# Projections, attention and routed experts of a two-layer block: statistics earlier, last values last, second product two behind, rows of maxima placed in one hop

## The reference

```python
h = _layernorm(x) * (1 + ca) + sa
Q, K, V = h @ W_q.T, h @ W_k.T, h @ W_v.T
Qr, Kr = _rope(Qh, cos, sin), _rope(Kh, cos, sin)
scores = einsum('bhqd,bhkd->bhqk', Qr, Kr) * DH ** (-0.5)       # causal
heads = einsum('bhqk,bhkd->bhqd', softmax(scores), Vh)
...
a = xf @ W1a_e + b1a_e                                          # for each expert e
b = xf @ W1b_e + b1b_e
y = silu(a) * b @ W2_e + b2_e
acc = acc + w_e[:, None] * y
```

## Time and profile before

| | us |
|---|---|
| median of 3 runs | 2507.34 (2504.72 to 2518.98) |
| the profiled execution | 2501.4 |
| its span | 2499.7 |
| PE busy | 2214.6 (89%) |
| DVE busy | 1692.3 (68%) |
| ACT busy | 1274.4 (51%) |
| POOL busy | 862.8 (35%) |

### The profile page before, as it was taken

One profiled execution on the slowest core, in us unless ns is written; L12 is line 12 of the kernel. 1 busy time (PEld: TensorE's weight loads), 2 busy tenths in 40 slices (PEclk: granted clock), 3 DMA queues, 4 the chain that ended last, 5 costly groups with the idle time before them and its releaser, 6 DMA issues. The chain is left out here.

```text
span 2499.7 us, 38782 instructions
## 1 busy us (share of the span) xinstructions
PE 2214.6 (89%) x12968; PEld 1404.3 (56%) x12968; DVE 1692.3 (68%) x2750; ACT 1274.4 (51%) x2452; POOL 862.8 (35%) x1057
## 2 busy tenths in 40 slices
PE   7876999999999999988999599963999999999991
PEld 5662333333333333326777456652888888888881
DVE  7767887878777787825787778764455555555456
ACT  2220777777766677773233244421455555555552
POOL 3442412213121211212455512444344434445341
PEclk9995999999999999998999798875999999999996
DMA  5389104042241500003000100115534434544326
GB/s 208 126 186 144 26 2 69 7 65 32 40 49 23 70 2 2 2 1 131 1 0 0 33 0 8 37 37 169 175 132 138 140 129 136 174 150 140 131 73 214
DMA packets 130021, 200.23 MB, mean 80 GB/s; under 512 B 13808, under 2 KB 102896, under 8 KB 128432
## 3 DMA queue, kind: packets, MB, share of 16 engines
q1 hardware_dynamic: 113472, 144.32, 17.3%
q0 software_dynamic: 14544, 48.05, 10.7%
q10 hardware_dynamic: 1824, 5.52, 1.3%
HBM read 150.97 MB, written 46.88 MB: 79 GB/s over the span
## 5 line engine op out<-in xcount | busy, mean ns | idle before, releaser
L917 DVE TENSOR_REDUCE tile_max<-p_m 128x2 f32<-128x1024 f32 (+3 forms) x640 | 651.4, 1061 | 146.1 <-PE p_m L779 76.4
L879 ACT ACTIVATE probs<-p_s 128x512 f32<-128x512 f32 (+3 forms) x1280 | 597.2, 535 | 244.9 <-PE p_s L788 240.2
L2143 PE MATMUL p_up<-f_xT,f_w 128*128 128x512 f32 (+1 forms) x2304 | 463.6, 350 | 9.2 <-POOL f_w L2306 9.2
L2143 PEld LDWEIGHTS p_up<-f_xT,f_w 128*128 128x128 f32 x2304 | 368.8, 189 | 59.6 <-issue 9.6
L725 POOL TENSOR_SCALAR_AFFINE_SELECT probs<-probs 128x128 f32<-128x128 f32 x512 | 145.0, 292 | 721.6 <-ACT probs L879 712.6
L775 PE MATMUL p_m<-ka,qa 96*128 96x512 bf16 (+3 forms) x1280 | 361.2, 365 | 30.9 <-PEq L256 18.5
L788 PE MATMUL p_s<-qa,ka 99*128 99x512 bf16 (+3 forms) x1280 | 351.6, 351 | 21.3 <-DMA qa<-max_scr 8.6
L2306 POOL TENSOR_TENSOR f_w<-f_raw,f_w 128x1024 fp32r<-128x1024 f32 x96 | 231.4, 2414 | 398.8 <-ACT f_w L2195 398.8
L802 PE MATMUL p_o<-probs,va 128*32 128x512 f32 (+3 forms) x2560 | 301.1, 541 | 0.3 <-POOL probs L725 0.3
L2158 PE MATMUL p_y<-f_w,f_hidden 128*128 128x256 f32 x1872 | 255.8, 283 | 28.7 <-DVE f_hidden L2260 14.9
L2158 PEld LDWEIGHTS p_y<-f_w,f_hidden 128*128 128x128 f32 x1872 | 237.3, 188 | 50.7 <-issue 31.5
(11 more groups left out here) (269 smaller groups left out, 2575.5 us busy)
## 6 DMA issues: line engine op xcount, KB each, us to landing
f_raw<-in_W1a SPq DMA_DIRECT2D x24, 1024.0 KB, 7.1
f_raw<-in_W1b SPq DMA_DIRECT2D x24, 1024.0 KB, 9.2
f_raw<-in_W SPq DMA_DIRECT2D x24, 1024.0 KB, 11.7
qk_scr<-parts SPq DMA_DIRECT2D x48, 256.0 KB, 2.8
qa<-qk_scr POOLq DMA_DIRECT2D x42, 256.0 KB, 15.6
ka<-qk_scr POOLq DMA_DIRECT2D x42, 256.0 KB, 17.5
v_scr<-wqkv_raw SPq DMA_DIRECT2D x32, 256.0 KB, 3.8
g_ys<-y_rows SPq DMA_DIRECT2D x16, 512.0 KB, 8.7
```

The costliest lines, as they stand in the source:

```text
L879: nc.scalar.activation(probs[:, (buf * UNITS + n) % NPROBS, h, lo:CH], p_s[:, s_bank(("exp", HG * n + h), buf), lo:CH], ACT.Exp, scale=DH ...
L917: nc.vector.tensor_reduce(out=tile_max[:, 2 * hp:2 * hp + 2, i, bank], in_=p_m[:, at_bank, :, 0:width], op=ALU.max, axis=AX.X).then_inc(ma ...
L2143: last = nc.tensor.matmul(p_up[:, f % 2, ab, 0:size], w1[:, wh, ab * KT + kt, f * P:(f + 1) * P], xT[:, t % 2, xh, kt, 0:size], start=(kt, ...
```

## The change

Four things are changed.

- In the projections the statistics of chunk i+2 stand behind `rest_of_hT(i + 1)` on DVE, the keys' two rotations are issued one ahead of and one behind `split(i, 0)`, and POOL's `deviation` stands ahead of the first `split_off`.
- In the last chunk PE multiplies the keys ahead of the values, ACT takes the values between the two roundings of the keys, and SP stores them between the queries' and the keys' parts.
- In the attention `place` is three DMAs straight from the rows in SBUF to the place under the queries, with one semaphore for each of the two row buffers; the scratch rows in DRAM go. ACT's next use of a row buffer waits for the placement, not for the store.
- In the experts the second product comes two blocks behind the first (`LAG`), `hidden` has three buffers, `take_y` stands behind the second `hide`, and the last two of the six pieces of weights change places.

```diff
 def store(i):
-    sp.wait_ge(va_ready, i + 1)
-    for hg in range(NHG):
-        sp.dma_start(k.v_scr[...], va[...]).then_inc(va_stored, 16)
     for qk in range(2):
+        if qk == last_chunk(i):
+            sp.wait_ge(va_ready, i + 1)
+            for hg in range(NHG):
+                sp.dma_start(k.v_scr[...], va[...]).then_inc(va_stored, 16)
         sp.wait_ge(last_part, 2 * i + qk + 1)
...
 def chunk(i, par):                              # POOL
     add(i, 0)
+    if i + 2 < NCH:
+        deviation(i + 2)
     split_off(i, 0)
     add(i, 1)
-    if i + 2 < NCH:
-        deviation(i + 2)
     split_off(i, 1)
...
-                    rotate(i, 0)                # DVE
+                    rotate(i, 0, range(2))
                     if not last_chunk(i):
                         rest_of_hT(i + 1, 1 - par)
-                    split(i, 0)
-                    rotate(i, 1)
                     if i + 2 < NCH:
                         statistics(i + 2)
+                    rotate(i, 1, range(1))
+                    split(i, 0)
+                    rotate(i, 1, range(1, 2))
...
                     nc.scalar.activation(parts[:, qk, 0, :, :], rem[:, qk, :, :], ACT.Copy).then_inc(rounded, 1)
+                    if last_chunk(i) and qk:
+                        take_v(i)
                     act.wait_ge(rem_ready, 2 * i + qk + 1)
...
-                    else:                       # PE, ahead of the values' product
+                    elif last_chunk(i):
+                        product(i, par, 1)
+                    if not first(i):
                         pe.wait_ge(va_ready, i)
...
                     if not last_chunk(i):
                         turn(i + 1)
-                    product(i, par, 1)
+                        product(i, par, 1)
...
                     sp.wait_ge(max_rows_ready, n + 1)
-                    sp.dma_start(k.max_scr[c % 2], max_rows[:, c % 2, :]).then_inc(max_stored, 16)
-                    sp.wait_ge(max_stored, 16 * n + 16)
-                    if not first(n):
-                        sp.wait_ge(max_placed, 16 * n)
-                    sp.dma_start(qa[buf][QROWS:QROWS + SPLIT, :, c * CH:(c + 1) * CH],
-                                 k.max_scr[c % 2].rearrange("(o h) t -> o h t", o=SPLIT)).then_inc(max_placed, 16)
+                    for o in range(SPLIT):
+                        sp.dma_start(qa[buf][QROWS + o:QROWS + o + 1, :, c * CH:(c + 1) * CH],
+                                     max_rows[o * HG:(o + 1) * HG, c % 2, :]).then_inc(max_placed[c % 2], 16)
...
-                            pe.wait_ge(max_placed, 16 * (CPS * s + c + 1))
+                            pe.wait_ge(max_placed[c % 2], PLACED * (CPS // 2 * s + c // 2 + 1))
...
+        LAG = 2
+        NHID = LAG + 1
-        hidden = m.sb("f_hidden", [P, 2, 2, ST], F32R)
+        hidden = m.sb("f_hidden", [P, NHID, 2, ST], F32R)
-        pieces = [(1, 0), (2, 0), (1, 1), (1, 2), (2, 1), (1, 3)]
+        pieces = [(1, 0), (2, 0), (1, 1), (1, 2), (1, 3), (2, 1)]
...
-                        if f:
-                            down(t, f - 1)
+                        if f >= LAG:
+                            down(t, f - LAG)
                         elif t:
-                            down(t - 1, FB - 1)
-                down(NTILES - 1, FB - 1)
+                            down(t - 1, FB + f - LAG)
+                for f in range(FB - LAG, FB):
+                    down(NTILES - 1, f)
...
-                        if n > 2:
-                            act.wait_ge(down_psum, n - 2)
+                        if n > NHID:
+                            act.wait_ge(down_psum, n - NHID)
...
-                        if f == 0 and t:
+                        if f == LAG - 1 and t:
                             take_y(t - 1)
```

## The result

The changed kernel takes 2474.6 us as the median of four runs (2474.0 to 2475.5), the kernel before on the same chip 2506.0. The medians differ by 31.4 us; the ratio over all runs is 0.986, with an interval of 0.984 to 0.989, which is 28 to 40 us of 2506. The forecast was 2474, with a sum of -33.2. The sum is right; two of its three terms are not, and that their errors cancel is luck. That is what the rest of this document is about.

A forecast was written before the change was run, and what follows sets the result against it. The prediction took a ring of waits to bound the projections, PE the attention and experts, and transfers the projections' end. Terms -14.7 - 6.5 - 12.0 = -33.2 gave 2468.2 on the profiled scale, 2474 as a median; range 2460 to 2493.

The forecast's parts named there:

- The ring of the projections: Projections: a chunk is a ring of waits, falling from 20.55 to 18.1 us; six intervals give -14.7.
- Steps 1 to 3: Projection chunk: statistics and L141 done by 4.2 us, POOL's power unnoticed, rotations around the split done by 7.7.
- Step 4: Projection chunk: normalization starts at 7.7 us, scalings end at 9.1, multiplication waits for split_off until 11.0, add ends 13.4.
- the scalings also take the port: Projections rival: scalings run after split_off or push it back, some 2.4 us a chunk; no gain there, 2489, chance 0.14.
- The one that has waited goes next: Projections, step 4: POOL's second add, waiting since 9.8 us, runs right after DVE's multiplication, 11.0 to 13.4.
- DVE keeping it: Projections rival: DVE keeps the port for multiplication and addition; 19.3 us a chunk, -7.5, total 2481, chance 0.18.
- POOL not being held: Projections rival: DVE doesn't hold POOL; 16.8 us a chunk, -22.5, total 2466, chance 0.15.
- The last stretch: End of projections: transfers hold it, so the last chunk's new order was counted as no gain.
- The placements: Attention: direct placement of the maxima's rows removes most of PE's 8.6 us of waits; -6.5.
- The experts: Routed experts: PE's 14.9 us of waits for hidden rows go, 0.5 stays, y costs 2.4; -12.0.
- The term for y: Experts: PE's wait for y grows 0.3 us in 8 short tiles, +2.4, bounds -9.7 and +7.
- The slower rival: Experts rival: take_y behind the second hide loses a POOL run of 2.4 us per tile; 2527, chance 0.04.

The follow-up runs named there:

- e5: The changed kernel with ACT doing the normalization's four scalings from chunk 2 on, the mean left out; ratio 0.983 to the kernel before.
- e1: The kernel before with only the new order of the projections' chunk; median 2499.2 against 2511.6 us, ratio 0.995.
- e9: e8 with POOL's second add ahead of its first split_off and DVE's last split between normalization's multiplication and addition; 2452.4 against 2507.6 us for the kernel before.
- e4: The kernel before with only the last chunk's new order; ratio 0.999 (0.998 to 1.001).
- e2: The kernel before with only the experts' part changed; ratio 0.992, experts 699.3 instead of 715.9 us.
- e6: The changed kernel with take_y between the second hide's two instructions; ratio 0.982 to the kernel before, experts 687.1 us.
- e7: The changed kernel with the normalization in eight fused DVE instructions instead of six, the last split in their middle; ratio 0.983 to the kernel before.
- e8: The changed kernel with ACT's scalings, now with the mean, and take_y between the second hide's instructions; 2453.4 against 2507.6 us for the kernel before, ratio 0.978.

## Why the prediction was right, and where it was wrong

- **The ring of the projections.** Steps 1 to 3 held: the statistics left the ring, L141 was short, the power ran unnoticed. Step 4 failed: I let the four scalings run to 9.1 unblocked, with the duration of L341, because shape and count are the same. They were held until 12.7 (84.31, with 71.58 as zero), and the add took the place I had given to the multiplication. Against e5, whose steps are those of the forecast, this costs 1.0 a chunk (18.65 and 17.66); the overlaps that steps 1 to 5 left out give back some 0.45, so that the forecast's 18.1 was off by 0.55 only. The six intervals gave 11.0 instead of 14.7: 1.7 in the first, where 19.6 was left to shorten, 1.9 in each of the next four, 1.7 in the last. The stage has -10.4, since its first chunk began 0.6 later in this execution; e1, whose first chunk began 0.6 earlier, has -11.3.
- **The row that I passed over.** L341 was the wrong neighbour: its row was alike in size, and nothing in it spoke of the port. L182 itself never met POOL in the kernel before. But another TENSOR_SCALAR with one tensor from SBUF did, beside the first POOL run of the earlier trace rows, in the same timeline:

```profile
1433.07 2.46 DVE L131 TENSOR_SCALAR y_sb<-y_sb 128x512 f32<-128x512 f32 x1
```

The same instruction takes 0.43 at 1439.5, with POOL idle. Two more that POOL holds stand at 1521.26 (L1757, 2.31) and 1742.25 (L2233, 2.18). So "two operands in SBUF" was too narrow a reading of the trace, and step 4 could have had a bound from both sides.

- **The rival that "the scalings also take the port"** had the right mechanism (0.41 to 2.50 each) and the wrong price: I let it cancel the whole gain, since I pushed back split_off by 2.4 and didn't follow the add. The held scalings take the turn that the multiplication would have had.
- **"The one that has waited goes next"** in step 4 is what e5 and e9 show: the add issued at 96.36 let the multiplication issued at 95.81 go first. The two rivals about the port, DVE keeping it and POOL not being held, fall with the same rows.
- **The last stretch** was right: transfers hold it (5.96 of wait left), e4 gives nothing.
- **The placements** were right: -6.5 forecast (half way between its ends of 4.9 and 8.6 would have been 6.75), -5.6 and -6.3 measured, with 0.5 and 0.8 of the waits left. One profile of this stage is good to some 4 us; by PE's idle time the seven kernels with the new placement are 4 to 8 ahead of the four others.
- **The experts** were right in mechanism and short in size. The term -14.9 came from PE's own list of waits, and each of these stops is some 0.2 longer in the weight loads: 22.7 for the hidden rows, of which 0.8 is left. Some 5 of it came back ahead of the up products, which the sum didn't have. So e2 shows -16.6 for the whole part where the sum had -12.0. The term for y, +2.4, measured +1.5, for the reason I gave (the second hide meets POOL's run in short tiles).
- **The slower rival** (take_y behind POOL in every tile) didn't come; y cost 14.3 in all, in 17 places, 1.6 more than before. Its mechanism, a second hide that POOL holds in front of take_y, shows in the short tiles (1.36 at 2034.21). The 11.1 of e6 are more than that price: they take out the whole wait for y, most of which the kernel before had too.
- **The scale.** I moved the sum by 5.9 from the profiled execution to the median. The profiled execution of the kernel before has, with e7, the shortest middle of eleven, so the move was right in kind. That 2474 meets 2474.6 to less than 1 us is luck all the same: the errors of the terms cancel, and the median of the kernel before was 2507.3 in three runs and 2506.0 in four. Where the middle's 6.5 went is told only in part, in the last section.

The Trainium skill (SBUF — State Buffer, Who interferes with whom) counts tensor_scalar among the operations that can take the pair of ports shared with GpSimd; the 2.50 of L182 agrees. I drew on another rule of the same section and passed this one over. It also says that issue order decides who blocks, which the turns in e5 and e9 agree with.

The Trainium skill (Perfetto Trace Analysis, Identifying the Most-Contended Engine) holds the busy share of the weight loads to be a better measure of how near TensorE is to its limit than that of the products, since these are pipelined. e2 agrees: with the same products PE's busy time fell by 6.5, that of the weight loads by 1.4.

## What to carry to other kernels

When work is moved to where another engine is busy, the price of each moved instruction needs a row in which that neighbour was active; a row of the same size with an idle neighbour is only one end of a range. Look for that row by the kind of operation, in the whole trace: here it stood in another layer. Where DVE and POOL share a ring, order both so that they take turns (e9: 16.9 a chunk instead of 18.65), and let ACT do what it can. Read PE's stops in the weight loads, where the same stop is some 0.2 us longer than in PE's row, and don't add the two lists. Place an instruction that PE will wait for ahead of one that POOL can hold.

## What the runs showed of the hardware

An instruction of DVE with one tensor from SBUF and two scalars per partition (L182, 128x256, 0.41 us) is held by POOL as one with two tensors is: 2.50 us at most. Four short ones lose more than one long one: each POOL instruction that ends lets about one of them in, so the four spanned two POOL runs (5.29), while the single multiplication of e5 got in after the first. Alone, a scaling and a subtraction of the same size (L2267, 128x256) both last about 0.41. Held, they differ: after POOL's end the scaling needs 0.15 more (12 cases in the kernel after, 0.148 to 0.155), the subtraction 0.28 (35 cases, 0.278 to 0.288).

The middle varied by 9 us between executions, without any change to it. The largest single piece is PE's wait for the experts' first rows: 20.8 in the kernel before, 25.2 to 28.0 in the ten other profiles. In front of that load stand stores into the same tensor, here four that SP issues (count, shortest/median/longest ns, first and last start), before and after:

```profile
L1458 SPq DMA_DIRECT2D x_slots<-u_sb x4: 332/342/363, 1712.2 to 1717.6; - x4
```

```profile
L1462 SPq DMA_DIRECT2D x_slots<-u_sb x4: 3/176/709, 1698.1 to 1709.7; - x4
```

The four issues stretched over 5.4 us in the one and 11.6 in the other (11.0 to 12.0 in all ten). What sets this I didn't try; and it isn't all, since e7 had a wait of 25.2 there and yet as short a middle as the kernel before. The granted clock goes with the rest: without that wait the middle is 590.5 to 592.8 in e6, e7 and e8, where its mean clock is 0.874 to 0.877, and 594.4 to 597.3 in the eight others, at 0.864 to 0.869. That the clock is the cause isn't shown.
